# Another order for the attention weights of layer 1: when ScalarE rectifies and exponentiates, and when VectorE masks

## The chip, the cores and the metric

The kernel runs on one core of one Trainium2 chip. The metric is the device time of one launch in microseconds (us); lower is better. Everything is computed in that one launch, from inputs in the chip's memory to the output there.

## The reference, cut to what matters

A batch of 8 graphs with 1024 nodes and 256 features goes through four layers, each followed by a residual sum and a layer normalisation. Layer 0 averages neighbours, layer 1 is the one that the change touches, layer 2 is three graph convolutions, layer 3 is attention with 8 heads. Layer 1:

```python
Xw = X @ Wv + bv
sj = Xw @ aw[:d, 0]
si = Xw @ aw[d:, 0]
e = leaky_relu(sj[:, None, :] + si[:, :, None] + ab[0], negative_slope=0.2)
alpha_matrix = A * exp(e)
transition = alpha_matrix / (sum(alpha_matrix, axis=-1, keepdims=True) + 1e-12)
for k in range(3):
    H = H + Xk @ Wk[k] + bk[k]
    Xk = einsum('bij,bjd->bid', transition, Xk)
return relu(H)
```

So for each of 1024 queries there are 1024 weights: a rectified sum of a query's scalar `si` and a key's scalar `sj`, its exponential, and the product with the adjacency `A` (the masking). The sum over the keys divides the products later.

## The kernel before

One loop over the 8 batch elements holds all four layers. The nodes are cut into 8 tiles of 128. There is no scheduler: each engine has its own list of instructions in an order written out by hand, and semaphores tie the lists together. An engine runs its list strictly in order, so an instruction that waits holds all behind it. Matrix products are made of three: each operand is split into a high part (`t_hi`, `u_hi`, `xt_hi`) and a rest (`t_lo`, `u_lo`, `xt_lo`), and TensorE multiplies high by high, high by rest and rest by high (lines 506 to 508).

In the stage of the change, a weight tile is named (part, t), with t the tile of queries. Parts 0 and 1 are the keys 0 to 511 and 512 to 1023 of the query tiles 0 to 3 (128 x 512 values each: the short tiles); part 2 is all keys of the tiles 4 to 7 (128 x 1024: the wide tiles). The list `AL` gives their order: (0,0) to (0,3), (1,0) to (1,3), (2,4) to (2,7), 12 in all. A tile goes through these steps:

- ScalarE: `leaky(part, t)` (line 1049) adds `si_col` to `sj_row` and rectifies into `al_area`; `exponential(part, t)` (line 1054) works in place and waits for the rectified values. `leaky_exp` is the two in a row. A rectifier also waits until `si` of its query tile is there, and where it writes again into a used buffer, until the old tile has been transposed. The first of part 1 waits for the second half of `sj_row`.
- VectorE: `weights(part, t)` (line 1371) multiplies by the adjacency in place and sums the row, into `rsum_a` for part 0 and into `rsum` for the others.
- TensorE: `transpose_alpha(part, t)` (line 605), 4 transposes of 128 x 128 for a short tile and 8 for a wide one, into PSUM.
- ScalarE: `al_transposed(part, t)` copies PSUM to `t_hi` (all copies have line 931, that of a helper).
- VectorE: its own `al_transposed(part, t)` writes `t_lo`, PSUM less `t_hi` (line 1228).
- TensorE: `hop(part, t)` multiplies the weights with the value rows, 12 matmuls for a short tile and 24 for a wide one. The first of them waits for `t_lo`.

TensorE's list runs one transposition ahead: `transpose_alpha(0, 2)`, `hop(0, 1)`, `transpose_alpha(0, 3)`, `hop(0, 2)` and so on to `transpose_alpha(2, 4)`, `hop(1, 3)`, `transpose_alpha(2, 5)`, `hop(2, 4)`.

The value rows are the projection of the normalised input with the weights `W_K2`, in four pairs of tiles. VectorE takes each pair from PSUM with `both_rows(k)`: a cast to `u_hi` (line 1385) and the difference to `u_lo` (line 1228). Pairs 2 and 3 are first used by `hop(1, 0)`. `s_j()` on VectorE (line 1363) writes the second half of `sj_row`. `s_i(b, t)` (line 1308) is the product of a normalised tile with a weight row, summed over the features into `si_col`; its full-size output is scratch, in `y`, `xr` or `si_out`. The semaphore `si_done` counts these.

The copies into `t_hi` wait once for `t_out`: the transposed adjacency, which stands in the same place, must have been written out to memory by the SyncE queue (it is loaded back for layer 2). After the stage, VectorE forms the reciprocals of the row sums, and TensorE goes on to the projections `z` and to the second product with the same weights.

Of the kernel before, what the change touches and what calls it, by code (L numbers as in the profile page):

```python
# [22 lines left out]
def build_program(nc: bass.Bass, d: dict, out: bass.AP):  # L23
    B, N, F = d["x"].shape
    NT = N // P
# [63 lines left out]
    with ExitStack() as ctx:  # L89
        def sb(name, shape, dt=F32, stack=ctx):  # L90
            return stack.enter_context(nc.sbuf_tensor(name, shape, dt))

        def sem(name):
            return ctx.enter_context(nc.semaphore(name))
# [14 lines left out]
        wsi_row = sb("wsi_row", [P, F])  # L109
# [6 lines left out]
        xn = sb("xn", [P, NT, F])  # L116
# [19 lines left out]
        with ExitStack() as s:  # L136
            t_cols = sb("t_cols", [P, N - F], F32, s)
            si_out = sb("si_out", [P, F], F32, s)
# [24 lines left out]
        with ExitStack() as s:  # L163
# [6 lines left out]
            xr = sb("xr", [P, 2, F], F32, s)  # L170
# [14 lines left out]
        with ExitStack() as s:  # L185
            y = sb("y", [P, 4, F], F32, s)
# [8 lines left out]
        def al(part, t):  # L195

            if part == 2:
                return al_area[:, 1 + (t - 3) % 3, :]
            at = N + (TPH * part + t) % 6 * 512
            return al_area[:, :, :].rearrange("p k n -> p (k n)")[:, at:at + 512]  # L200
# [39 lines left out]
        si_done = sem("si_done")  # L240
# [43 lines left out]
        def nth(b, per, n):  # L284

            return b * per + n
# [40 lines left out]
        def al_banks(part, t):  # L327

            banks = BANKS[tp["al", part, t]]
            return ps[:, banks[0]:banks[-1] + 1, :].rearrange("p h (j i) -> p (h j) i", i=P)  # L330

        def al_keys(part):

            return slice(0, NT) if part == 2 else slice(TPH * part, TPH * (part + 1))

        def hop_place(t):

            return ps[:, ACC + t % 4, t // 4 * F:(t // 4 + 1) * F]
# [591 lines left out]
        def _(act):  # L930
# [79 lines left out]
            for b in range(B):  # L1010
# [23 lines left out]
                def leaky(part, t):  # L1034

                    n = AL.index((part, t))
                    act.wait_ge(si_done, nth(b, NT, t + 1))
                    if n == 0:
                        act.wait_ge(y_ready, nth(b, 3 * NT, NT))
                        act.wait_ge(sj_act, b + 1)  # L1040
                    if n == TPH:
                        act.wait_ge(pr_free, nth(b, PR_UNITS, pr["sj", 1] + 1))
                    if 6 <= n < 8:
                        act.wait_ge(tp_full, nth(b, TP_UNITS, tp["al", 0, n - 6] + 1))
                    elif n >= 8:
                        before = [("al", 0, 3), ("al", 1, 1), ("al", 1, 3), ("al", 2, 4)][n - 8]
                        act.wait_ge(tp_full, nth(b, TP_UNITS, tp[before] + 1))
                    row = sj_row[:, :] if part == 2 else sj_row[:, part * 512:(part + 1) * 512]
                    act.activation(al(part, t), row, ACT.Prelu, bias=si_col[:, t:t + 1], scale=1.0,
                                   alpha=SLOPE).then_inc(e_lin, 1)  # L1050

                def exponential(part, t):
                    act.wait_ge(e_lin, nth(b, len(AL), AL.index((part, t)) + 1))
                    act.activation(al(part, t), al(part, t), ACT.Exp).then_inc(e_exp, 1)

                def leaky_exp(part, t):
                    leaky(part, t)
                    exponential(part, t)

                def al_transposed(part, t):  # L1060
                    act.wait_ge(tp_full, nth(b, TP_UNITS, tp["al", part, t] + 1))
                    copy(t_hi[:, al_keys(part), t * P:(t + 1) * P], al_banks(part, t)).then_inc(tp_hi, 1)
# [10 lines left out]
                x_late_transposed(b, 1, 2)  # L1073
                exponential(0, 0)
                leaky_exp(0, 1)
                leaky(0, 2)
                act.wait_ge(t_out, nth(b, 32 * NT, 32 * NT))
                al_transposed(0, 0)
                exponential(0, 2)
                al_transposed(0, 1)  # L1080
                leaky_exp(0, 3)
                al_transposed(0, 2)
                leaky_exp(1, 0)
                al_transposed(0, 3)
                leaky_exp(1, 1)
                al_transposed(1, 0)
                leaky_exp(1, 2)
                al_transposed(1, 1)
                leaky_exp(1, 3)
                al_transposed(1, 2)  # L1090
                leaky(2, 4)
                al_transposed(1, 3)
                exponential(2, 4)
                leaky_exp(2, 5)
                for t in range(TPH, NT):
                    al_transposed(2, t)
                    if t + 2 < NT:
# [98 lines left out]
        def _(dve):  # L1196

            dve.wait_ge(set_in, SET_LOADS)
            for n, slot in enumerate((W_L0X, W_L0G, W_Q, W_K, W_V, W_O)):
                dve.wait_ge(set_act, n + 1)  # L1200
                scale = QSCALE if slot == W_Q else 1.0
                dve.scalar_tensor_tensor(out=w_lo[:, slot, :, :].rearrange("p k o -> p (k o)"),
                                         in0=ps[:, TP + n % 2, :], scalar=scale,
                                         in1=f32(w_hi[:, slot, :, :].rearrange("p k o -> p (k o)")),
# [17 lines left out]
            def alone():  # L1222

                dve.sem_inc(passed, 1)

            def rest(dst, value, hi, done):

                dve.tensor_tensor(dst, value, f32(hi), ALU.subtract).then_inc(done, 1)  # L1228
# [73 lines left out]
            def s_i(b, t):  # L1302

                dve.wait_ge(ln_done, nth(b, LN_PER, t + 1))
                if t == NT - 1:
                    dve.wait_ge(si_done, nth(b, NT, NT - 1))
                alone()
                dve.tensor_tensor_reduce(out=y[:, t % 4, :] if t < NT - 3 else (xr[:, 0, :] if t == NT - 3 else si_out[:, :]), in0=xn[:, t, :], in1=wsi_row[:, :], scale=1.0, scalar=0.0,
                                         op0=ALU.mult, op1=ALU.add, accum_out=si_col[:, t:t + 1]).then_inc(si_done, 1)

            def hidden(b, c):
# [8 lines left out]
            for b in range(B):  # L1320
# [16 lines left out]
                for t in range(NT):  # L1337
# [4 lines left out]
                                             scalar=rdeg[:, t:t + 1], in1=ev[:, t % 2, 0:F], op0=ALU.mult,  # L1342
# [23 lines left out]
                def weights(part, t):  # L1366

                    dve.wait_ge(e_exp, nth(b, len(AL), AL.index((part, t)) + 1))
                    alone()
                    keys = slice(0, N) if part == 2 else slice(part * 512, (part + 1) * 512)  # L1370
                    dve.tensor_tensor_reduce(out=al(part, t), in0=al(part, t), in1=adjn[:, t, keys], scale=1.0, scalar=0.0,  # L1371
                                             op0=ALU.mult, op1=ALU.add,
                                             accum_out=(rsum if part else rsum_a)[:, t:t + 1]).then_inc(al_ready, 1)

                def al_transposed(part, t):

                    at = slice(t * P, (t + 1) * P)
                    dve.wait_ge(tp_hi, nth(b, TP_UNITS, tp["al", part, t] + 1))
                    rest(t_lo[:, al_keys(part), at], al_banks(part, t), t_hi[:, al_keys(part), at], tp_free)

                def both_rows(k):

                    n, at = pr["v", k], slice(k * 512, (k + 1) * 512)
                    dve.wait_ge(pr_full, nth(b, PR_UNITS, n + 1))
                    dve.tensor_copy(u_hi[:, at], ps[:, PR + n % 2, :]).then_inc(v_hi, 1)  # L1385
                    if k == 0:
                        dve.wait_ge(sj_act, b + 1)
                        dve.sem_inc(pr_free, 1)
                    dve.wait_ge(v_hi, nth(b, PAIRS, k + 1))
                    rest(u_lo[:, at], ps[:, PR + n % 2, :], u_hi[:, at], pr_free)  # L1390
# [7 lines left out]
                weights(0, 1)  # L1398
                s_j()
                al_transposed(0, 0)  # L1400
                s_i(b, NT - 3)
                both_rows(3)
                weights(0, 2)
                al_transposed(0, 1)
                weights(0, 3)
                al_transposed(0, 2)
                weights(1, 0)
                al_transposed(0, 3)
                weights(1, 1)
                al_transposed(1, 0)  # L1410
# [20 lines left out]
                for k in range(NT // 2 + 1):  # L1431
                    if k < NT // 2:
# [3 lines left out]
                        for s in range(2):  # L1436
                            t = 2 * k + s
                            last = dve.scalar_tensor_tensor(
                                out=ev[:, k % 2, 512 + s * F:512 + (s + 1) * F],
                                in0=hop_place(t), scalar=rdeg[:, t:t + 1],  # L1440
                                in1=ev[:, k % 2, s * F:(s + 1) * F], op0=ALU.mult, op1=ALU.add)
# [5 lines left out]
                for t in range(NT + 1):  # L1447
                    if t < NT:
# [7 lines left out]
                                                 scalar=rdeg[:, t:t + 1], in1=ev[:, t % 2, 0:F], op0=ALU.mult,  # L1456
# [45 lines left out]
                for k, part in enumerate(QK):  # L1502
# [4 lines left out]
                    if k == 7:  # L1507
# [5 lines left out]
                                             scalar=cols[:, 2 + m, ft:ft + 1], in1=f32(qk_place(part, u_hi, qk0_hi)),  # L1513
                                             op0=ALU.add, op1=ALU.subtract).then_inc(pr_free, 1)
                stacks_copied(range(G + 1, 3 * G + 2, 2))
                for s in range(UNITS + 13):
                    if s < UNITS:
# [4 lines left out]
                        if s >= 4:  # L1522
# [3 lines left out]
                            out=r[:, s % RSLOTS, :], in0=ps[:, 2 * (s % 2):2 * (s % 2) + 2, :].rearrange("p a c -> p (a c)"),  # L1526
                            in1=adjn[:, qt, :], scale=1.0, scalar=-3.0e38, op0=ALU.mult, op1=ALU.max,
# [73 lines left out]
```

## Time and profile before

| | before |
|---|---|
| time, median of 3 runs | 3142.06 us (3141.99 to 3142.89) |
| the profiled execution | 3141.49 us, span 3139.7 us |
| TensorE matmul busy (PE) | 3023.2 us, 96% |
| TensorE weight load busy (PEld) | 2645.5 us, 84% |
| VectorE busy (DVE) | 2090.6 us, 67% |
| ScalarE busy (ACT) | 1724.4 us, 55% |
| GpSimd busy (POOL) | 448.6 us, 14% |
| mean granted TensorE clock | 0.992 of full speed |
| DMA | 234.50 MB, mean 75 GB/s |

The profile is of one execution. Its span is the time from the first to the last instruction, 1.8 us under the time of that execution. Busy time of an engine says how much work it has, not whether the end waits for it; matmuls are pipelined, so a start every 0.12 us with a duration of 0.28 us each is normal. What is decisive for an engine that is nearly always busy are its gaps: the views of the waits and of the timeline show how long it stood idle before an instruction and what released it. "L605" is line 605 of the kernel; an instruction's text gives the tile written, then the tiles read, their shapes, and how many were merged in one row.

### The profile page before, as it was taken

What the parts mean: (1) busy time and instruction counts of PE and PEld (TensorE: products, weight loads), DVE (VectorE), ACT (ScalarE), POOL (GpSimd) and SP (SyncE); (2) the same over time, 40 slices, a digit from 0 to 9 for tenths busy, and PEclk for the clock granted to TensorE, in tenths of its full rate; (3) what the DMA queues carried; (4) which work ended last, traced back from release to release, by engine and by line L of the source; (5) the groups of instructions that cost most, each with busy time, mean ns of one, the idle gap of its engine ahead of it and who ended that gap; (6) DMA issues with size and microseconds to landing.
All of it is one profiled execution on the core that took longest, in us unless ns stands there. A gap on an engine that the chain in (4) does not pass through costs nothing.

```text
span 3139.7 us, 71133 instructions
## 1 busy us (share of the span) xinstructions
PE 3023.2 (96%) x28188; PEld 2645.5 (84%) x28188; DVE 2090.6 (67%) x4060; ACT 1724.4 (55%) x3048; POOL 448.6 (14%) x1666
## 2 busy tenths in 40 slices
PE   6999999999999999999999999999999999999999
PEld 5988789877898788987889877898778987789877
DVE  4637976379762797627976389753887538874388
ACT  3525855258542684526844278442784337853377
POOL 0101211012110121101211012111121111211112
PEclk9999999999999999999999999999999999999999
DMA  5022131121321213202133021330213302133010
GB/s 218 30 79 65 49 145 54 57 70 44 144 77 37 67 52 135 96 22 67 49 135 108 12 71 44 134 108 14 69 52 125 108 14 72 49 125 108 24 42 19
DMA packets 145270, 234.50 MB, mean 75 GB/s; under 512 B 12839, under 2 KB 113964, under 8 KB 144940
## 3 DMA queue, kind: packets, MB, share of 16 engines
q1 hardware_dynamic: 144940, 229.96, 22.3%
q8 instruction: 225, 3.69, 0.5%
q14 instruction: 105, 0.86, 0.1%
HBM read 120.86 MB, written 83.89 MB: 65 GB/s over the span
## 4 chain that ended last, share of the span: by engine, by line
PE 87%; DVE 7%; ACT 3%; issue 2%; SPq 1%; POOL 1%; DMA 0%; DVEq 0%; POOLq 0%; ACTq 0%
PE ps L506 16%; PE ps L508 16%; PE ps L507 16%; PE ps L734 15%; PE ps L724 9%; PE ps L752 8%; PE ps L605 1%; DVE t_lo L1228 1%; PE ps L765 1%; PE ps L564 1%; PE ps L595 1%; DVE al_area L1371 1%; DVE u_hi L1385 1%; ACT t_hi L931 1%; PE ps L705 0%
## 5 line engine op out<-in xcount | busy, mean ns | idle before, releaser
L1525 DVE CUSTOM_DVE_ANT_0 r<-ps,adjn 128x1024 f32<-128x1024 f32 x512 | 620.7, 1212 | 18.9 <-DVE xr L1572 10.3
L1172 ACT ACTIVATE r<-r,nmax 128x1024 f32<-128x1024 f32 x512 | 584.8, 1142 | 23.0 <-POOL nmax L498 22.3
L506 PE MATMUL ps<-u_hi,t_hi 128*128 128x256 f32 x2048 | 588.6, 287 | 0.6
L508 PE MATMUL ps<-u_hi,t_lo 128*128 128x256 f32 x2048 | 579.3, 283 | 0.0
L507 PE MATMUL ps<-u_lo,t_hi 128*128 128x256 f32 x2048 | 578.9, 283 | 0.0
L734 PEld LDWEIGHTS ps<-ident,r 128*128 128x128 f32 x4096 | 462.5, 141 | 115.4 <-issue 77.4
L734 PE MATMUL ps<-ident,r 128*128 128x128 f32 x4096 | 536.8, 274 | 7.2 <-DVE pt L1541 7.0
L1541 DVE COPY pt<-ps 128x512 f32<-128x512 f32 x512 | 352.9, 689 | 93.4 <-PE ps L734 73.8
L931 ACT ACTIVATE pt<-ps 128x512 f32<-128x512 f32 x512 | 304.0, 594 | 176.5 <-PE ps L734 158.2
L506 PEld LDWEIGHTS ps<-u_hi,t_hi 128*128 128x128 f32 x2048 | 391.5, 191 | 4.0 <-DVE t_lo L1228 4.0
L507 PEld LDWEIGHTS ps<-u_lo,t_hi 128*128 128x128 f32 x2048 | 391.4, 191 | 0.0
L508 PEld LDWEIGHTS ps<-u_hi,t_lo 128*128 128x128 f32 x2048 | 391.2, 191 | 0.0
L724 PE MATMUL ps<-k_stack,q_stack 96*128 96x512 f32 x1024 | 363.3, 437 | 6.2 <-ACT k_stack L931 4.3
L1006 ACT ACTIVATE xn<-y,shift,rstd 128x256 f32<-128x256 f32 x192 | 115.6, 602 | 456.7 <-POOL shift L474 455.9
L506 PE MATMUL ps<-w_hi,xt_hi 128*128 128x256 f32 x1152 | 334.2, 290 | 18.1 <-DVE xt_lo L1235 8.2
L507 PE MATMUL ps<-w_lo,xt_hi 128*128 128x256 f32 x1152 | 322.8, 280 | 0.0
L508 PE MATMUL ps<-w_hi,xt_lo 128*128 128x256 f32 x1152 | 322.5, 280 | 0.0
L467 POOL TENSOR_TENSOR vare<-mv,eps_ln 128x1 f32<-128x1 f32 x256 | 53.5, 209 | 1607.6 <-DVE mv L1289 1607.6
L752 PE MATMUL ps<-pt,xn 128*32 128x128 f32 x8192 | 274.9, 275 | 0.0
L1228 DVE TENSOR_TENSOR xt_lo<-ev,xt_hi 128x512 fp32r<-128x512 f32 x64 | 44.3, 693 | 316.4 <-ACT xt_hi L931 316.4
L506 PEld LDWEIGHTS ps<-w_hi,xt_hi 128*128 128x128 f32 x1152 | 218.2, 189 | 35.6 <-issue 12.5
L498 POOL TENSOR_TENSOR nmax<-zero,mmax 128x1 f32<-128x1 f32 x512 | 97.1, 190 | 1036.7 <-DVE mmax L1525 1013.8
(165 smaller groups left out, 5237.2 us busy)
## 6 DMA issues: line engine op xcount, KB each, us to landing
adjn<-in_adj SPq DMA_DIRECT2D x64, 512.0 KB, 3.4
t_spill<-t_hi SPq DMA_DIRECT2D x64, 512.0 KB, 5.9
t_spill<-t_lo SPq DMA_DIRECT2D x64, 512.0 KB, 6.0
t_hi<-t_spill SPq DMA_DIRECT2D x32, 1024.0 KB, 5.4
t_lo<-t_spill SPq DMA_DIRECT2D x32, 1024.0 KB, 8.1
xn<-in_x SPq DMA_DIRECT2D x16, 512.0 KB, 4.2
x_spill<-xn SPq DMA_DIRECT2D x64, 128.0 KB, 1.7
q_stack<-u_hi SPq DMA_DIRECT2D x64, 128.0 KB, 2.5
```

What stands on the lines that cost most here:

```text
L498: pool.tensor_tensor(nmax[:, u % 4:u % 4 + 1], zero[:, :], mmax[:, u % 4:u % 4 + 1], ALU.subtract).then_inc(neg_max, 1)
L506: pe.matmul(dst, a_hi, b_hi, start=first, stop=False, skip_group_check=check)
L507: pe.matmul(dst, a_hi, b_lo, start=False, stop=False, skip_group_check=check)
L508: return pe.matmul(dst, a_lo, b_hi, start=False, stop=last, skip_group_check=check)
L724: last = pe.matmul(ps[:, 2 * (u % 2) + half, :], q_stack[0:STACK, h, qt * P:(qt + 1) * P], k_stack[0:STACK, h, half * 512:(half + 1) * 512 ...
L734: last = pe.transpose(ps[:, TP + half, t * P:(t + 1) * P], r[:, u % RSLOTS, (TPH * half + t) * P:(TPH * half + t + 1) * P], ident)
L752: last = pe.matmul(ps[HD * hh:HD * (hh + 1), ctx_bank(grp), g * P:(g + 1) * P], xn[:, kt, h * HD:(h + 1) * HD], p_half(grp * G + hh, kt // ...
L931: copy = lambda dst, src, scale=1.0: nc.scalar.activation(dst, src, ACT.Copy, scale=scale)
L1006: act.activation(dst, src, ACT.Identity, bias=shift[:, t % 4:t % 4 + 1], scale=rstd[:, t % 4:t % 4 + 1]).then_inc(ln_done, 1)
L1172: act.activation(r[:, s % RSLOTS, :], r[:, s % RSLOTS, :], ACT.Exp, bias=nmax[:, s % 4:s % 4 + 1], accum_out=prow[:, qt % 2, h:h + 1]).the ...
L1525: dve.tensor_tensor_reduce(out=r[:, s % RSLOTS, :], in0=ps[:, 2 * (s % 2):2 * (s % 2) + 2, :].rearrange("p a c -> p (a c)"), in1=adjn[:, q ...
L1541: dve.tensor_copy(p_half(u, 0).rearrange("p t q -> p (t q)"), ps[:, TP, :]).then_inc(p_dve, 1)
```

## The change

On ScalarE, the steps of the short tiles and of the first two wide ones come in another order. Before, most tiles have `leaky_exp` in one piece between two copies. After, (0,2) is done in full and (0,3) rectified before the first copy; from there each gap between two copies holds the exponential of one tile and the rectifier of the next. (2,4) is rectified ahead of copy (1,1) and exponentiated ahead of copy (1,2), (2,5) rectified ahead of copy (1,3) and exponentiated behind it.

On VectorE, `both_rows(3)` goes from ahead of `weights(0, 2)` to behind `weights(0, 3)`, and `s_i(b, NT - 3)` from ahead of `both_rows(3)` to behind `weights(1, 0)`. The scratch output of `s_i(b, NT - 3)` goes to `si_out`, as that of the two after it, no longer to `xr`; so `s_i(b, NT - 2)` too waits for the one before it. No instruction on data is added or taken away, and TensorE's, GpSimd's and SyncE's lists are as they were.

```diff
--- before.py
+++ after.py
@@ -1073,25 +1073,30 @@
                 x_late_transposed(b, 1, 2)
                 exponential(0, 0)
                 leaky_exp(0, 1)
-                leaky(0, 2)
+                leaky_exp(0, 2)
+                leaky(0, 3)
                 act.wait_ge(t_out, nth(b, 32 * NT, 32 * NT))
                 al_transposed(0, 0)
-                exponential(0, 2)
+                exponential(0, 3)
+                leaky(1, 0)
                 al_transposed(0, 1)
-                leaky_exp(0, 3)
+                exponential(1, 0)
+                leaky(1, 1)
                 al_transposed(0, 2)
-                leaky_exp(1, 0)
+                exponential(1, 1)
+                leaky(1, 2)
                 al_transposed(0, 3)
-                leaky_exp(1, 1)
+                exponential(1, 2)
+                leaky(1, 3)
                 al_transposed(1, 0)
-                leaky_exp(1, 2)
+                exponential(1, 3)
+                leaky(2, 4)
                 al_transposed(1, 1)
-                leaky_exp(1, 3)
+                exponential(2, 4)
                 al_transposed(1, 2)
-                leaky(2, 4)
+                leaky(2, 5)
                 al_transposed(1, 3)
-                exponential(2, 4)
-                leaky_exp(2, 5)
+                exponential(2, 5)
                 for t in range(TPH, NT):
                     al_transposed(2, t)
                     if t + 2 < NT:
@@ -1302,10 +1307,10 @@
             def s_i(b, t):
 
                 dve.wait_ge(ln_done, nth(b, LN_PER, t + 1))
-                if t == NT - 1:
-                    dve.wait_ge(si_done, nth(b, NT, NT - 1))
+                if t > NT - 3:
+                    dve.wait_ge(si_done, nth(b, NT, t))
                 alone()
-                dve.tensor_tensor_reduce(out=y[:, t % 4, :] if t < NT - 3 else (xr[:, 0, :] if t == NT - 3 else si_out[:, :]), in0=xn[:, t, :], in1=wsi_row[:, :], scale=1.0, scalar=0.0,
+                dve.tensor_tensor_reduce(out=y[:, t % 4, :] if t < NT - 3 else si_out[:, :], in0=xn[:, t, :], in1=wsi_row[:, :], scale=1.0, scalar=0.0,
                                          op0=ALU.mult, op1=ALU.add, accum_out=si_col[:, t:t + 1]).then_inc(si_done, 1)
 
             def hidden(b, c):
@@ -1398,13 +1403,13 @@
                 weights(0, 1)
                 s_j()
                 al_transposed(0, 0)
-                s_i(b, NT - 3)
-                both_rows(3)
                 weights(0, 2)
                 al_transposed(0, 1)
                 weights(0, 3)
+                both_rows(3)
                 al_transposed(0, 2)
                 weights(1, 0)
+                s_i(b, NT - 3)
                 al_transposed(0, 3)
                 weights(1, 1)
                 al_transposed(1, 0)
```

## Rows read from the trace of the kernel before

**Rows 1.** The page: busy time and share by engine; the last chain by engine.

```profile
PE 3023.2 (96%) x28188; PEld 2645.5 (84%) x28188; DVE 2090.6 (67%) x4060; ACT 1724.4 (55%) x3048; POOL 448.6 (14%) x1666
...
PE 87%; DVE 7%; ACT 3%; issue 2%; SPq 1%; POOL 1%; DMA 0%; DVEq 0%; POOLq 0%; ACTq 0%
```

**Rows 2.** TensorE's waits, whole span: who waited for whom, us in total, times, longest.

```profile
PE ps L605 <- DVE rsum L1371: 13.0, 8, 1.6
...
PE ps L605 <- DVE rsum_a L1371: 4.4, 8, 0.6
```

**Rows 3.** TensorE's timeline, third element: start, us, instruction, count, idle before and its releaser.

```profile
874.75 0.60 PE L605 MATMUL ps<-ident,al_area 128*128 128x128 f32 x4
...
875.10 0.37 PE L506 MATMUL ps<-u_hi,t_hi 128*128 128x256 f32 x1
...
877.31 0.66 PE L605 MATMUL ps<-ident,al_area 128*128 128x128 f32 x4 [0.54 <-DVE rsum_a L1371]
...
877.91 0.39 PE L506 MATMUL ps<-u_hi,t_hi 128*128 128x256 f32 x1
...
879.45 0.60 PE L605 MATMUL ps<-ident,al_area 128*128 128x128 f32 x4
...
886.91 0.60 PE L605 MATMUL ps<-ident,al_area 128*128 128x128 f32 x4
...
890.56 1.09 PE L605 MATMUL ps<-ident,al_area 128*128 128x128 f32 x8 [1.63 <-DVE rsum L1371]
...
892.92 1.03 PE L605 MATMUL ps<-ident,al_area 128*128 128x128 f32 x8
...
894.04 0.39 PE L506 MATMUL ps<-u_hi,t_hi 128*128 128x256 f32 x1
...
897.01 1.03 PE L605 MATMUL ps<-ident,al_area 128*128 128x128 f32 x8
...
897.81 0.36 PE L506 MATMUL ps<-u_hi,t_hi 128*128 128x256 f32 x1
```

**Rows 4.** ScalarE's timeline, third element.

```profile
865.79 0.60 ACT L1006 ACTIVATE xn<-y,shift,rstd 128x256 f32<-128x256 f32 x1 [3.96 <-POOL shift L474]
...
866.30 0.67 ACT L1068 ACTIVATE sj_row<-ps,e_const 128x512 f32<-128x512 f32 x1
...
871.19 0.63 ACT L1054 ACTIVATE al_area<-al_area 128x512 f32<-128x512 f32 x1
...
871.73 0.71 ACT L1049 ACTIVATE al_area<-sj_row,si_col 128x512 f32<-128x512 f32 x1
...
873.41 0.60 ACT L931 ACTIVATE t_hi<-ps 128x512 fp32r<-128x512 f32 x1 [0.98 <-PE ps L605]
...
873.91 0.62 ACT L1054 ACTIVATE al_area<-al_area 128x512 f32<-128x512 f32 x1
...
886.17 1.14 ACT L1049 ACTIVATE al_area<-sj_row,si_col 128x1024 f32<-128x1024 f32 x1
...
887.54 0.60 ACT L931 ACTIVATE t_hi<-ps 128x512 fp32r<-128x512 f32 x1 [0.23 <-PE ps L605]
...
888.04 1.05 ACT L1054 ACTIVATE al_area<-al_area 128x1024 f32<-128x1024 f32 x1
```

**Rows 5.** VectorE's timeline, third element.

```profile
873.63 0.75 DVE L1363 TENSOR_SCALAR sj_row<-ps,e_const 128x512 f32<-128x512 f32 x1
...
875.23 0.69 DVE L1385 CAST u_hi<-ps 128x512 fp32r<-128x512 f32 x1
...
876.56 0.68 DVE L1371 CUSTOM_DVE_ANT_0 al_area<-al_area,adjn 128x512 f32<-128x512 f32 x1
...
877.17 0.69 DVE L1228 TENSOR_TENSOR t_lo<-ps,t_hi 128x512 fp32r<-128x512 f32 x1
...
877.77 0.68 DVE L1371 CUSTOM_DVE_ANT_0 al_area<-al_area,adjn 128x512 f32<-128x512 f32 x1
...
889.27 1.23 DVE L1371 CUSTOM_DVE_ANT_0 al_area<-al_area,adjn 128x1024 f32<-128x1024 f32 x1 [2.10 <-ACT al_area L1054]
```

## What I expect of the change, and why

> **What bounds the kernel now.** I read the page's busy shares and its chain by engine first [rows 1]: TensorE is busy 96% of the span and carries 87% of the chain that ended last. Time can come out only where TensorE stands still. The view of who waited for whom, for TensorE, then gives the stops of the edited stage [rows 2]: the transposes of line 605 waited for VectorE's `rsum` 8 times, 13.0 us in all, and for its `rsum_a` 8 times, 4.4 us in all. Eight is once per batch element, and the longest single waits (1.6 us, 0.6 us) are about the means, so all elements behave alike. I follow the third one, by TensorE's timeline [rows 3], then ScalarE's [rows 4] and VectorE's [rows 5], because a wait says who came last, not why.
>
> I write T(p,t) for a tile's transposes on TensorE, hop(p,t) for its matmuls, leaky, exp and copy for ScalarE's three steps, w for VectorE's masking and rest for its `t_lo` subtraction. With nothing late a short cycle (T, then a hop) takes (886.91 - 879.45) / 4 = 1.865 us, its T 0.35 of it (874.75 to 875.10), so its hop 1.515. A wide T takes 0.80 (897.01 to 897.81). Against these TensorE loses [rows 3]:
> - First wait: T(0,2) could start at 875.10 + 1.515 = 876.62 and starts at 877.31: 0.69.
> - hop(0,1) follows 0.60 behind that T, not 0.35: 0.25.
> - Second wait: T(2,4) could start at 886.91 + 1.865 = 888.78 and starts at 890.56: 1.78.
> - hop(2,4) starts at 894.04, where 892.92 + 0.80 = 893.72 was possible: 0.32.
>
> Together 3.04 us an element, 24.3 us over eight: no reordering in this stage can gain more.
>
> **Why the long wait is there.** ScalarE starts leaky(2,4) at 886.17, then copies (1,3) at 887.54, for which it waits until T(1,3) is done, and only then runs exp(2,4), 888.04 to 889.09 [rows 4]. w(2,4) follows at 889.27 and takes 1.23 [rows 5]; T(2,4) starts 0.06 later [rows 3]. So the exponential stands behind a copy that cannot be early.
>
> **The ScalarE edit, step by step.** No instruction is added or removed; 12 rectifiers, 12 exponentials and 12 copies stay. Start to start, one behind the other [rows 4]: exp to the next 0.54 (871.19 to 871.73), copy to the next 0.50 (873.41 to 873.91), leaky to its own exp 0.74, since it waits for that result (871.19 + 0.54 + 0.74 gives the exp of the new order at 872.47). The new order also has leaky followed by a copy. Before shows this pair only where the copy waited for TensorE (886.17 and 887.54 in [rows 4]), with 0.23 us idle at most; an upper bound is that it costs as much as to its own exp, 0.74, a lower one is what another ScalarE step with column operands shows: the normalisation of 0.60 is followed after 0.51 (865.79, 866.30), an overlap of 0.09, so 0.71 - 0.09 = 0.62. I take 0.62, as that row is the same kind of instruction without a wait.
>
> The Trainium skill, "ScalarE: Activation LUTs", section "What ACT_TABLE_LOAD costs", says that back-to-back ACTIVATEs overlap by about 93 ns, which is what the row of the normalisation shows; by that rule the sum is the one with 0.62, and without it the one with 0.74 below.
>
> From leaky(0,2) at 871.73 [rows 4]: exp(0,2) 872.47, leaky(0,3) 873.01, copy(0,0) 873.63. That copy is 0.22 later than before. Its rest started at 874.29, 0.60 + 0.03 behind the copy's end is 874.26, so what follows is not later. Then exp(0,3) 874.13, and leaky(1,0) 874.67, which now stands ahead of copy(0,1) and needs the second half of `sj_row`: VectorE writes it 873.63 to 874.38 [rows 5], cover 0.29. copy(0,1) starts at 875.39, right behind T(0,1) (874.75 + 0.60), as before.
>
> **The VectorE edit.** Before, `s_i(b, NT - 3)` and the value pair (`both_rows(3)`: cast at 875.23, its difference, next instruction at 876.56, so 1.33) stand ahead of w(0,2), 876.56 to 877.24 [rows 5], and that is the first wait. After, w(0,2) follows rest(0,0) at 874.90 (exp(0,2) was done at 873.10) and ends at 875.58, over 1 us before TensorE could use it. rest(0,1) at 876.02 (copy end 875.99) ends at 876.71: hop(0,1) can start at 876.97. Both losses go, 0.94. What is late next: w(0,3) at 876.62 takes 0.61 to the next instruction, then the value pair 1.33, so rest(0,2) starts at 878.56 and ends at 879.25; hop(0,2) could start at 876.62 + 1.865 + 0.35 = 878.83 and gets its data at about 879.30. A new wait of 0.47, behind the moved pair. Net of this edit with the ScalarE edit: hop(0,2) at 879.30, where before T(0,3) at 879.45 puts it at 879.80, a gain of 0.50. The value pair is needed first by hop(1,0) four cycles on; `s_i(b, NT - 3)` only by leaky(2,5). The extra wait on `si_done` ahead of `s_i(b, NT - 2)` is for an instruction several steps back; w(1,2), next in line behind it, ends some 0.8 us before T(1,2) needs it. No DMA and nothing of SyncE or GpSimd moves; the SyncE queue waits for TensorE's later products and shifts with them.
>
> **The rest of the stage.** From hop(0,2) at 879.30 the cycles run at 1.865: T(1,0) 880.82, T(1,1) 882.68, T(1,2) 884.55, T(1,3) 886.42, T(2,4) 888.29. Does w(2,4) keep up? ScalarE's short cycle is 0.62 + 0.50 + 0.54 = 1.66 (1.78 by the upper bound), under 1.865. exp(2,4) comes at about 884.0 and ends at 885.1, ahead of copies (1,2) and (1,3). VectorE needs 0.60 for a rest and 0.61 for a w [rows 5], is free of rest(1,2) at 886.42 and ends w(2,4) at 887.65, 0.64 ahead of need. The second wait goes; T(2,4) is 890.56 - 888.29 = 2.27 earlier. copy(1,3) starts 0.65 behind T(1,3), at 887.07; exp(2,5) follows at 887.57, 1.05 long, then w(2,5) 0.18 later, 888.81 to 890.04; T(2,5) wants it at 888.29 + 0.80 + 1.515 = 890.61, cover 0.57. At hop(2,4) the way of a wide tile (T, copy, rest) took 894.04 - 890.56 = 3.48 before; TensorE's own work in it is 0.80 + 1.515 + 0.80 = 3.12. This wait stays, 0.31 to 0.36. From there the orders agree. hop(2,4) comes at 891.72, a gain of 2.32 an element.
>
> **The sum.** 8 x 2.32 = 18.6 us. The profiled execution took 3141.49 us (span 3139.7); after, 3122.9. The median of the runs is 3142.06, 0.6 above, which gives 3123.5. With 0.74 for leaky to copy, copies (0,1), (0,2) and (1,1) come up to 0.3 late, the gain is 2.10 an element, 16.8 us, and the time is 3125.3. TensorE's granted clock is 0.992 of full speed on the mean of the span, so next to always at the higher of its two levels; idle time only goes away, and I cost the clock at nothing.
>
> **Rivals.**
> 1. *The moved pair eats the first gain.* If rest(0,2) is late by 0.5 more than I work out (VectorE reading TensorE's banks more slowly when denser work runs, or copy(0,1) late behind leaky(1,0), whose cover is 0.29), only the second wait is won: 8 x 1.78 = 14.2, 3127.9. For it: VectorE has no slack between 876.0 and 879.3 in the new order. Against: each step is a duration read in this stage.
> 2. *Both waits go with no new one.* Adds 8 x 0.47: 22.3, 3119.8. Against: 0.47 has to be made up on a full VectorE.
> 3. *The work moved makes no difference to the end:* the time is given back later, at a transfer or at the products behind the stage. [Rows 2] has no transfer that this stage's TensorE work waits for. About 3142, within 6 us.
> 4. *Slower: ScalarE becomes the bound.* If a rectifier, an exponential and a copy no longer run pairwise but cost more one by one, as with a change of function, the copies hold every hop. The point at which the whole gain is gone is a ScalarE cycle of 1.865 + 2.32 / 8 = 2.16 where I have 1.66; each 0.1 beyond costs 8 x 8 x 0.1 = 6.4 us. A step to 2.4 gives some 3157. Against: 871.19 to 871.73, 873.41 to 873.91 and the 0.23 idle at most at 887.54 [rows 4] are such changes, and none shows a pause.
>
> The same page of the Trainium skill, section "Table sets: the hidden batching unit", tells to batch by table set since a switch costs about 2.7 us; that would speak for the fourth rival by far, but the pairs in these rows show no such switch.
>
> **How the numbers follow.** Forecast 0.71, first rival 0.16, second 0.04, third 0.05, fourth 0.04. Predicted 3123.5. A change of under 0.2% (6.3 us) can't be told from none here. The forecast's own range is 3121 to 3126; with the first two rivals' ends the range is 3119.7 to 3128.2. Faster 0.71 + 0.16 + 0.04 = 0.91, same 0.05, slower 0.04.
>
> **What would show it.** After: no wait of line 605 for `rsum` or `rsum_a`; in its place a wait of line 506 for `t_lo`, some 0.5 us an element at hop(0,2), plus the 0.3 at hop(2,4) that stays; copies spaced 1.87 in the short cycles; `al_area` of (2,4) exponentiated before copy(1,2). Wrong if line 605 still waits for VectorE, or if `t_lo` waits appear in several cycles per element.

## The result and the profile after

| | before | after |
|---|---|---|
| time, median of 5 runs | 3142.06 us (3141.32 to 3143.99) | 3125.73 us (3123.78 to 3131.49) |
| the profiled execution, span | 3141.49 us, 3139.7 us | 3123.78 us, 3122.0 us |
| the stage, in each element | 34.45 to 34.47 us | 32.08 to 32.13 us |

The ratio is 0.995, with a 95% interval of 0.9938 to 0.9962: faster, by 16.3 us on the medians and 17.7 us between the two profiled executions. Timed again beside the kernel before, the changed one took 3123.62 us against 3142.66 (ratio 0.9937, 0.9925 to 0.995). "The stage" is here and below the time from the start of the activation that writes the first half of `sj_row` (line 1068) to the first transpose of the last wide tile, T(2,7). It is read from the two timelines, as the mean of the 8 elements, and is the length that the change acts on.

The page of the changed kernel: its span, the busy times, and the chain that ended last by engine.

```profile
span 3122.0 us, 71133 instructions
...
PE 3021.2 (97%) x28188; PEld 2645.0 (85%) x28188; DVE 2089.0 (67%) x4060; ACT 1718.1 (55%) x3048; POOL 448.6 (14%) x1666
...
PE 87%; DVE 5%; ACT 3%; SPq 2%; issue 1%; POOL 1%; DMA 0%; DVEq 0%; POOLq 0%; ACTq 0%
```

TensorE runs the same 28188 matmuls with 2.0 us less of busy time, in a span 17.7 us shorter; the gain is idle time. TensorE's waits, who waited for whom, us in total, times and longest:

```profile
PE ps L564 <- DVE t_lo L1233: 23.4, 8, 3.2
...
PE ps L506 <- DVE t_lo L1233: 1.8, 8, 0.3
```

Line 605 has no row any more, where [rows 2] had 13.0 and 4.4 us. A wait of line 506 for `t_lo` is new, once per element. The other wait, at line 564, was there before and has nothing to do with the stage. TensorE's timeline of the third element (in all timelines: start, us, instruction, count, idle before and its releaser; beside [rows 3]):

```profile
871.57 0.60 PE L605 MATMUL ps<-ident,al_area 128*128 128x128 f32 x4
...
873.44 0.60 PE L605 MATMUL ps<-ident,al_area 128*128 128x128 f32 x4
...
873.79 0.36 PE L506 MATMUL ps<-u_hi,t_hi 128*128 128x256 f32 x1
...
875.31 0.60 PE L605 MATMUL ps<-ident,al_area 128*128 128x128 f32 x4
...
876.12 0.39 PE L506 MATMUL ps<-u_hi,t_hi 128*128 128x256 f32 x1 [0.22 <-DVE t_lo L1233]
...
877.65 0.60 PE L605 MATMUL ps<-ident,al_area 128*128 128x128 f32 x4
...
883.25 0.60 PE L605 MATMUL ps<-ident,al_area 128*128 128x128 f32 x4
...
885.12 0.71 PE L605 MATMUL ps<-ident,al_area 128*128 128x128 f32 x5
...
887.43 0.71 PE L605 MATMUL ps<-ident,al_area 128*128 128x128 f32 x5
...
888.53 0.38 PE L506 MATMUL ps<-u_hi,t_hi 128*128 128x256 f32 x1
...
891.50 0.71 PE L605 MATMUL ps<-ident,al_area 128*128 128x128 f32 x5
```

The figure x4 or x5 counts the transposes that the view merged in one row. The rows are T(0,1), T(0,2), the start of hop(0,1), T(0,3), the start of hop(0,2), T(1,0), T(1,3), T(2,4), T(2,5), the start of hop(2,4), T(2,6). T(0,2) follows T(0,1) after 1.87 and T(2,4) follows T(1,3) after 1.87, a plain cycle both times: the two long waits are gone. hop(0,2) starts 0.81 behind T(0,3), where 0.35 would do, and hop(2,4) 1.10 behind T(2,5), where 0.80 would do. The view of the waits shows less of this than the distances from start to start: it has 0.22 us at hop(0,2), where the start is 0.46 late, and nothing at hop(2,4), since the ends of the matmuls ahead are modelled. The distances are what counts here.

ScalarE (beside [rows 4]):

```profile
869.83 0.71 ACT L1049 ACTIVATE al_area<-sj_row,si_col 128x512 f32<-128x512 f32 x1
...
870.45 0.58 ACT L931 ACTIVATE t_hi<-ps 128x512 fp32r<-128x512 f32 x1
...
880.82 1.06 ACT L1054 ACTIVATE al_area<-al_area 128x1024 f32<-128x1024 f32 x1
...
882.02 0.60 ACT L931 ACTIVATE t_hi<-ps 128x512 fp32r<-128x512 f32 x1
...
883.89 0.60 ACT L931 ACTIVATE t_hi<-ps 128x512 fp32r<-128x512 f32 x1 [0.23 <-PE ps L605]
```

leaky(0,3) to copy(0,0) takes 0.62. exp(2,4) runs at 880.82, ahead of copies (1,2) and (1,3), which are the last two rows. VectorE (beside [rows 5]): w(0,2), w(0,3), the cast of the last value pair, rest(0,2), w(2,4).

```profile
871.72 0.68 DVE L1376 CUSTOM_DVE_ANT_0 al_area<-al_area,adjn 128x512 f32<-128x512 f32 x1
...
873.45 0.68 DVE L1376 CUSTOM_DVE_ANT_0 al_area<-al_area,adjn 128x512 f32<-128x512 f32 x1
...
874.05 0.69 DVE L1390 CAST u_hi<-ps 128x512 fp32r<-128x512 f32 x1
...
875.38 0.68 DVE L1233 TENSOR_TENSOR t_lo<-ps,t_hi 128x512 fp32r<-128x512 f32 x1
...
883.26 1.22 DVE L1376 CUSTOM_DVE_ANT_0 al_area<-al_area,adjn 128x1024 f32<-128x1024 f32 x1
```

w(0,2) now ends over 1 us ahead of T(0,2). Between w(0,3) and rest(0,2) stands the value pair, and rest(0,2) ends at 876.06, 0.06 ahead of the late hop(0,2). w(2,4) ends at 884.48, 0.64 ahead of T(2,4).

### The profile page after: what moved, and what is told of

It is laid out like the page before. It is cut to its first block, busy times and chain, and to the rows that moved or that the text cites. A ratio compares the mean times of both kernels' runs of the same rounds, so it can differ in the third digit from the quotient of the medians.

```text
span 3122.0 us, 71133 instructions
## 1 busy us (share of the span) xinstructions
PE 3021.2 (97%) x28188; PEld 2645.0 (85%) x28188; DVE 2089.0 (67%) x4060; ACT 1718.1 (55%) x3048; POOL 448.6 (14%) x1666
## 4 chain that ended last, share of the span: by engine, by line
PE 87%; DVE 5%; ACT 3%; SPq 2%; issue 1%; POOL 1%; DMA 0%; DVEq 0%; POOLq 0%; ACTq 0%
PE ps L506 17%; PE ps L508 16%; PE ps L507 16%; PE ps L734 15%; PE ps L724 9%; PE ps L752 8%; DVE t_lo L1233 2%; SPq L409 1%; PE ps L605 1%; PE ps L765 1%; PE ps L564 1%; ACT t_hi L931 1%; PE ps L595 1%; DVE xt_lo L1240 0%; DVE stats L1289 0%
```

## The experiments

All stages are the means over the 8 elements of the profiled execution. Times are medians, and "before" is the median of the kernel before on the same chip; the rows come from two chips, so gains are to be compared by the ratios and not by the medians.

| kernel | stage, us | time, us | before, us | ratio, 95% interval |
|---|---|---|---|---|
| before | 34.46 | | | |
| after | 32.11 | 3123.62 | 3142.66 | 0.9937 (0.9925 to 0.995) |
| ScalarE's order alone | 32.60 | 3126.94 | 3141.71 | 0.9951 (0.9938 to 0.9965) |
| VectorE's order alone | 34.76 | 3144.32 | 3141.71 | 1.0009 (1.0 to 1.0018) |
| value pair parted | 31.63 | 3117.69 | 3141.71 | 0.9924 (0.9911 to 0.9936) |
| one swap in the kernel before | 34.03 | 3137.45 | 3141.71 | 0.9985 (0.9977 to 0.9994) |
| after, ScalarE loaded | 33.36 | 3133.98 | 3142.66 | 0.9969 (0.9958 to 0.9981) |
| value pair parted, wide tile in halves | 31.37 | 3118.66 | 3142.66 | 0.9922 (0.9908 to 0.9935) |

**ScalarE's order alone.** The kernel before with the new ScalarE list of the diff.

> Only ScalarE's new order; VectorE's list as before. The stage is measured from the start of the first `sj_row` activation to the last wide T of an element: 34.46 us before, 32.11 after the whole change. My theory (each wait is the meeting of three in-order lists; the two edits are not additive): the first wait stays as it is (T(0,2) about 0.7 late, hop(0,1) 0.24), the second, at T(2,4), goes, hop(2,4) keeps 0.3. Stage 32.6, gain 1.87 an element, 15 us in all, about 3127. Rival (the long wait needs both edits, since VectorE's masking comes late): T(2,4) still waits for over 0.5, stage over 33.1.

The stage is 32.60, as worked out. TensorE's waits of line 605:

```profile
PE ps L605 <- DVE rsum_a L1376: 4.4, 8, 0.6
```

The wait for `rsum_a`, the first one, is whole (4.4 us), and the wait for `rsum`, the second one, is gone, without VectorE's edit. 1.86 of the 2.35 us an element is ScalarE's.

**VectorE's order alone.** The kernel before with the new VectorE list and the scratch place that goes with it.

> Only VectorE's new order (and the scratch place that goes with it); ScalarE's list as before. My theory: T(0,2) is no longer late, but exp(0,3) still stands behind copy(0,1), so w(0,3), the value pair behind it and then rest(0,2) are late, and hop(0,2) waits 1.3; the second wait stays whole. Stage 34.8, slower than before by 0.3 an element, 3 us in all, about 3145. Rival (additive: the first wait belongs to VectorE's order alone): stage 33.5 to 34.0, 4 to 8 us faster.

The stage is 34.76, 0.30 longer than before; on the totals the interval reaches 1.0, so 2.6 us slower is at the edge of what they tell, and the stage tells it in all 8 elements (34.74 to 34.80). The waits:

```profile
PE ps L605 <- DVE rsum L1371: 13.0, 8, 1.6
...
PE ps L506 <- DVE t_lo L1228: 8.3, 8, 1.0
```

The wait for `rsum_a` is gone and one for `t_lo` has come in its place, 8.3 us where 4.4 went. ScalarE (copy(0,1), leaky(0,3), exp(0,3)), VectorE (w(0,3), rest(0,2)) and TensorE (T(0,3), hop(0,2)) show the way:

```profile
877.38 0.60 ACT L931 ACTIVATE t_hi<-ps 128x512 fp32r<-128x512 f32 x1 [0.80 <-PE ps L605]
...
877.88 0.71 ACT L1049 ACTIVATE al_area<-sj_row,si_col 128x512 f32<-128x512 f32 x1
...
878.62 0.63 ACT L1054 ACTIVATE al_area<-al_area 128x512 f32<-128x512 f32 x1
```

```profile
879.43 0.69 DVE L1371 CUSTOM_DVE_ANT_0 al_area<-al_area,adjn 128x512 f32<-128x512 f32 x1 [0.73 <-ACT al_area L1054]
...
881.38 0.68 DVE L1228 TENSOR_TENSOR t_lo<-ps,t_hi 128x512 fp32r<-128x512 f32 x1
```

```profile
880.49 0.60 PE L605 MATMUL ps<-ident,al_area 128*128 128x128 f32 x4
...
882.12 0.39 PE L506 MATMUL ps<-u_hi,t_hi 128*128 128x256 f32 x1 [1.03 <-DVE t_lo L1228]
```

exp(0,3) stands behind copy(0,1) and ends at 879.25; w(0,3) starts 0.18 later, the value pair behind it, and rest(0,2) ends at 882.06. So hop(0,2) starts 1.63 behind its T. VectorE's half of the edit is worth 0.49 on top of ScalarE's (32.60 to 32.11) and costs 0.30 without it. This half moves two things, `s_i(b, NT - 3)` and the value pair, and no run moves one alone. By [rows 5] the pair alone would do for the first wait: w(0,2) would then start at 875.23 and end at 875.91, ahead of the 876.62 at which T(0,2) could start. That is an estimate.

**The last value pair parted.** The changed kernel, with `both_rows(3)` cut in its two instructions, the cast (`high_rows`) and the difference (`low_rows`):

```diff
                 weights(0, 2)
+                high_rows(3)
                 al_transposed(0, 1)
                 weights(0, 3)
-                both_rows(3)
+                low_rows(3)
                 al_transposed(0, 2)
```

> The changed kernel with one more step: the last value pair's two instructions on VectorE are parted, the cast goes to where VectorE waits for copy(0,1) (behind w(0,2)), the difference stays behind w(0,3). My theory: the 0.47 at hop(0,2) is the cast's place in VectorE's line and nothing else; it goes, no new wait comes. Stage 31.65, 0.47 less than after the change, 3.7 us in all, about 3121. Rival (VectorE simply has too much work between two hops): the wait moves to hop(0,3) or hop(1,0), stage 32.0 to 32.2.

The stage is 31.63, and the wait for `t_lo` at line 506 has no row left. VectorE (w(0,2), cast, rest(0,1), w(0,3), the pair's difference, rest(0,2)), then TensorE (T(0,3), hop(0,2)):

```profile
869.70 0.68 DVE L1376 CUSTOM_DVE_ANT_0 al_area<-al_area,adjn 128x512 f32<-128x512 f32 x1
...
870.30 0.68 DVE L1390 CAST u_hi<-ps 128x512 fp32r<-128x512 f32 x1
...
870.91 0.68 DVE L1233 TENSOR_TENSOR t_lo<-ps,t_hi 128x512 fp32r<-128x512 f32 x1
...
871.50 0.68 DVE L1376 CUSTOM_DVE_ANT_0 al_area<-al_area,adjn 128x512 f32<-128x512 f32 x1
...
872.11 0.68 DVE L1233 TENSOR_TENSOR u_lo<-ps,u_hi 128x512 fp32r<-128x512 f32 x1
...
872.72 0.68 DVE L1233 TENSOR_TENSOR t_lo<-ps,t_hi 128x512 fp32r<-128x512 f32 x1
```

```profile
873.23 0.60 PE L605 MATMUL ps<-ident,al_area 128*128 128x128 f32 x4
...
873.58 0.36 PE L506 MATMUL ps<-u_hi,t_hi 128*128 128x256 f32 x1
```

The cast fills the time in which VectorE waited for copy(0,1), and hop(0,2) starts 0.35 behind its T. The pair also costs less in two pieces, 0.61 and 0.61, where together it took 1.33: the difference waits for the cast's result, and right behind it that wait shows. So the new wait of the changed kernel was one instruction's place, not too much work on VectorE.

**One swap.** The kernel before, with the exponential taken ahead of the copy that stood in front of it:

```diff
                 leaky(2, 4)
-                al_transposed(1, 3)
                 exponential(2, 4)
+                al_transposed(1, 3)
                 leaky_exp(2, 5)
```

> The kernel before with a single swap: exp(2,4) ahead of copy(1,3), nothing else. My theory: the exponential comes only 0.7 earlier, since ScalarE is behind already (its short cycle of 1.78 leaves 0.09 of TensorE's 1.865), so T(2,4) still waits about 1.1 and copy(1,3), now late, makes w(2,5) and T(2,5) wait 0.3. Stage 34.0, gain 0.45 an element, 3 to 4 us in all, about 3138. Rival (the long wait is that one swap): stage about 32.7, over 12 us faster.

The stage is 34.03. T(1,3), T(2,4) and T(2,5):

```profile
885.76 0.60 PE L605 MATMUL ps<-ident,al_area 128*128 128x128 f32 x4
...
888.73 0.77 PE L605 MATMUL ps<-ident,al_area 128*128 128x128 f32 x5 [0.95 <-DVE rsum L1371]
...
891.34 0.77 PE L605 MATMUL ps<-ident,al_area 128*128 128x128 f32 x5
```

T(2,4) comes 2.97 behind T(1,3), where 1.865 would do, so it is late by 1.11 instead of 1.78, and T(2,5) comes 2.61 behind T(2,4), where 0.80 + 1.515 = 2.32 would do. The copy that the timeline shows ahead of the late exponential is little over a third of the 1.78; the rest is that ScalarE arrives at leaky(2,4) with no lead, and the run with ScalarE's order alone, where T(2,4) follows T(1,3) after 1.87, shows that a lead removes all of it.

**ScalarE loaded.** The changed kernel with more work on ScalarE in part 1:

```diff
+                    if part == 1:
+                        copy(al(part, t), row).then_inc(extra, 1)
+                        act.wait_ge(extra, 4 * b + t + 1)
                     act.activation(al(part, t), row, ACT.Prelu, bias=si_col[:, t:t + 1], scale=1.0,
```

> The changed kernel with more work on ScalarE: ahead of each rectifier of part 1 a plain copy of the same size into the buffer that the rectifier then overwrites, and a wait for it; by the durations of after about 0.65 us more in each of four short cycles. The result is the same. My theory: ScalarE's cycle of 1.66 has only 0.2 to spare against TensorE's 1.865, so these 2.6 us make several hops wait (hop(0,1), (0,2), (0,3), (1,0), (1,1), together about 1.7 more than after), and the last idle of ScalarE takes up the rest. Stage 33.5, against 32.11, 11 us in all, about 3137. Rival (VectorE alone is the limit in the new order, ScalarE has slack): stage 32.1 to 32.4, under 3 us.

The stage is 33.36: 1.25 longer than after, for about 2.6 us of work. ScalarE's cycle, from copy(0,1) over exp(1,0), the added copy and leaky(1,1) to copy(0,2):

```profile
874.77 0.58 ACT L932 ACTIVATE t_hi<-ps 128x512 fp32r<-128x512 f32 x1
...
875.25 0.62 ACT L1058 ACTIVATE al_area<-al_area 128x512 f32<-128x512 f32 x1
...
875.77 0.62 ACT L932 ACTIVATE al_area<-sj_row 128x512 f32<-128x512 f32 x1
...
876.42 0.72 ACT L1053 ACTIVATE al_area<-sj_row,si_col 128x512 f32<-128x512 f32 x1
...
877.05 0.58 ACT L932 ACTIVATE t_hi<-ps 128x512 fp32r<-128x512 f32 x1
```

It is 2.28 long, against TensorE's 1.865, and no step of it is idle. The loss was expected as 1.4, 0.14 too much. This is the fourth rival's mechanism made real: where ScalarE's cycle goes above TensorE's, the hops wait, and 1.66 leaves 0.2.

**The first wide tile in halves.** On top of the parted pair, ScalarE copies (2,4) in two halves of 512, and VectorE subtracts the first while the second is copied:

```diff
+                    if (part, t) == (2, TPH):
+                        at = slice(t * P, (t + 1) * P)
+                        copy(t_hi[:, 0:TPH, at], al_banks(part, t)[:, 0:TPH, :]).then_inc(first_hi, 1)
+                        copy(t_hi[:, TPH:NT, at], al_banks(part, t)[:, TPH:NT, :]).then_inc(tp_hi, 1)
+                        return
```

(VectorE's `al_transposed` likewise.)

> The previous kernel with the parted value pair, and the first wide tile (2,4) copied and subtracted in two halves of 512, so that VectorE starts on the first while ScalarE copies the second. My theory: the 0.3 at hop(2,4) is the length of the line T, copy, rest (3.43 against TensorE's own 3.12 in it); by halves it is about 2.95, and the wait goes. Stage 31.3 to 31.4, 0.75 less than after the change, 6 us in all, about 3119. Rival (the two more instructions on each engine, about 0.1 each, cost at T(2,6) what they give): stage 31.6 to 31.7.

T(2,5), hop(2,4), T(2,6), hop(2,5):

```profile
885.19 0.71 PE L606 MATMUL ps<-ident,al_area 128*128 128x128 f32 x5
...
885.98 0.36 PE L507 MATMUL ps<-u_hi,t_hi 128*128 128x256 f32 x1
...
888.94 0.71 PE L606 MATMUL ps<-ident,al_area 128*128 128x128 f32 x5
...
889.79 0.39 PE L507 MATMUL ps<-u_hi,t_hi 128*128 128x256 f32 x1
```

hop(2,4) starts 0.79 behind T(2,5), so its wait is gone; hop(2,5) has 0.05 of a new one. The stage is 31.37. The first totals (3118.66 against 3117.69, beside different runs of before) did not show it, so the two were run again side by side.

> The kernel with the parted value pair, side by side with the one with halves on the same chip. Stage 31.63 as in its first run. Median 3116 to 3121.

> The kernel with the parted value pair and the first wide tile in halves, on the same chip. Stage 31.36, 0.27 an element less, so 2.2 us less by the stages; the medians should differ by that if enough runs average out the stretch between elements, whose length varies by about 2 us from element to element in every kernel. Rival: no difference or slower by the totals, as in the first comparison (3117.69 and 3118.66), which would mean that the halves cost elsewhere what they give here.

Stages 31.63 and 31.36; medians 3117.16 (3115.95 to 3118.32) and 3116.22 (3111.98 to 3117.35), ratios to before 0.9922 (0.9909 to 0.9934) and 0.9913 (0.99 to 0.9927). Over the 8 elements the stages differ by 2.2 us in sum; the totals now point the same way, where the first comparison pointed the other, and can't confirm it. Both beat the changed kernel. Against the kernel before on the same chip the parted pair gained 24.0 and 24.4 us and the kernel with halves 24.0 and 25.4, where the changed kernel gained 16.3 and 19.0; by the stages they should gain 3.8 and 5.9 us more than it. What exceeds that is not explained by the stage.

**The changed kernel again.**

> The changed kernel itself, timed again beside the kernel before. The stage is 32.11 in every element. If the scatter of its times (3123.8 to 3131.5, against 2.7 us for the kernel before) lies between the end of attention and the next element's first products, where TensorE's granted clock falls in some elements, then the stretches outside that one repeat within 0.1 us here too, and the median may be anywhere from 3122 to 3128. Rival (the new order itself varies): the stage's length differs between elements by over 0.3.

The stage was 32.06 to 32.14 in all elements, so the new order itself doesn't vary. From T(2,7) to the first scores of layer 3 it was 150.57 to 150.63. From there to the next element's stage the lengths were 200.98 to 202.68. That stretch holds the scatter, in every kernel. Over the first five kernels' profiles (before, after twice, parted, ScalarE alone), 35 such stretches, its length goes with the granted clock of 20 us around the end of an element: about 201.0 on the mean of the three where no drop shows (1.00), 202.0 at 0.91, 202.5 at 0.83. But within the level of 0.91 alone the lengths run from 200.96 to 203.21, so the clock can't be the whole of it. Two such stretches of the changed kernel, the shortest (200.44) and the longest (203.21), each 20 us from 148.04 behind the first scores on; columns are the stretch, its length, busy time and instructions of PE, PEld, DVE, ACT and POOL, granted clock, DMA share, GB/s:

```profile
1193.90:1213.90 20.00, 15.13 (x122) 13.77 (x123) 14.21 (x26) 12.09 (x24) 1.94 (x7) 1.00 0.81 311
...
2731.60:2751.60 20.00, 14.67 (x106) 12.90 (x106) 14.03 (x28) 10.96 (x22) 2.73 (x9) 0.91 0.74 276
```

In both, TensorE is idle for a quarter of the time and DMA carries the next adjacency. The counts of instructions show that the two windows don't hold the same work: the longer stretch is already 1.9 us behind where its window starts, so their GB/s can't be set against each other.

Counting TensorE's matmuls (transposes among them) from the first scores on gives pieces of equal work, and two of them hold 2.4 of the 2.77 us.

- *The first 80, at the start of layer 3:* 12.53 us in the shorter stretch, 14.07 in the longer, at the full clock in both. In the longer one TensorE waits twice here for VectorE's `pt` (line 1546), 1.2 us together; the shorter has no such wait over 0.13 us.
- *The 60 from number 1901 on, around the end of the element:* 11.78 us at a clock of 1.00 over the 20 us, 12.68 at 0.91. A matmul takes 0.282 us on the mean in the one and 0.314 in the other, TensorE's idle time is shorter in the longer one (3.50 against 3.95 us), and DMA moves 250 and 260 GB/s. So this part goes with the clock: the matmuls themselves run longer, and DMA is no slower.

The eleven profiles bear this out, in the 75 of their 77 stretches that show the same number of matmuls. The second piece takes 11.73 to 11.79 us at 1.00 (5 stretches), 12.18 to 12.68 at 0.91 (51) and 13.07 to 13.42 at 0.83 (19), with nothing in between. The first piece takes 12.53 to 14.14, whatever the clock does later. The two pieces between them vary by 0.4 us each, and the last 39 us before the next stage by 0.1. What makes VectorE late at the start of layer 3 no run here tells. Nor does any trace show the slowest execution of the changed kernel, 3131.49 us, which was not profiled.

## Why the prediction was right, point by point

- *TensorE's gaps are the only source.* Right: the instructions are the same, and of the stage's 2.35 us an element (34.46 to 32.11) 2.28 are the gaps that went and came (0.69 + 0.25 + 1.78 - 0.46 + 0.02). The prediction left out a small one: behind the late T(2,4) the next T came after 2.36 ([rows 3], 890.56 to 892.92), where 0.80 + 1.515 = 2.32 would do; after the change it comes after 2.31. So the 3.04 us that it called the most a reordering could gain were some 0.05 too low; parted pair and halves together gain 3.09, though the halves add instructions.
- *First wait.* T(0,2) late by 0.69 and hop(0,1) by 0.25: both gone. The new wait at hop(0,2) was forecast at 0.47; it is 0.81 - 0.35 = 0.46. Its cause was named right too: parting the value pair removed it.
- *Leaky to copy, between 0.62 and 0.74.* Measured 0.62 at copy(0,0). The rule of the Trainium skill about back-to-back activations ("ScalarE: Activation LUTs", section "What ACT_TABLE_LOAD costs") holds in this trace: 0.71 for the rectifier, 0.62 to the next start. No pause at a change of function shows either.
- *Second wait.* Forecast gone, with w(2,4) 0.64 ahead; measured 0.64. The ScalarE list alone removes it.
- *hop(2,4) keeps 0.31 to 0.36.* Measured 1.10 - 0.80 = 0.30, just under that.
- *Gain of 2.32 an element.* Measured 2.35; over eight, 18.8 us against 18.6.
- *The total.* Forecast 3122.9 for a profiled execution and 3123.5 for the median; measured 3123.78 and 3125.73. What differs lies outside the stage. Between the two profiled executions the stages gave 18.83 us. Of the rest, the start of the first stage came 1.48 later (94.36 against 92.88), the stretch behind the last T(2,7) took 0.6 more, the middle parts 0.2 more and the seven stretches between elements 1.1 less, about half of it in each of the two pieces named above: 17.7 in all. The prediction counted these at nothing and had no range for them. In the eleven profiles the span less the eight stages is 2862.9 to 2866.5 us, 2864.0 in the kernel before and 2864.6 on the mean of the ten others, so nothing is a fair mean and some 2 us either way would have been a fair range for one execution; the profile before already showed the stretches between elements to differ by 1.9 us. The first median of five came out 2.2 us above the forecast, near the upper end of its own range (3121 to 3126), the second, 3123.62, 0.1 above. How near a single median falls is luck.
- *The rivals.* The first (only the second wait is won, 14.2 us) didn't come; ScalarE's list alone is close to it, 1.86 x 8 = 14.9. The second (no new wait) did not come with this change and is what the parted pair does: 8 x 2.83 = 22.6 us by the stages, where it was put at 22.3. The third is out: of the 18.8 us that the stages gained, 17.7 arrived at the end of the profiled execution, and the rest is within the scatter outside them. The fourth needs a ScalarE cycle of 2.16; loaded to 2.28 in four cycles the kernel was still faster than before (0.9969). Only four of the eight short cycles were loaded; an estimate for all eight, 8 x (2.28 - 1.865) = 3.3 us an element, is more than the whole gain of 2.35.
- *What I did not say:* that VectorE's edit alone is slower than the kernel before. The prediction costed both edits in one order, and its statement of the first wait reads as if VectorE's list alone removed it. The run shows that it only does so together with exp(0,3) ahead of the first copy.

## What to carry to other kernels

Where each engine follows its own fixed list, write down the start of each step on each engine for one round, with intervals read from the trace; here that gave the stage's length within 0.05 us for the change and five further variants, and within 0.14 us for the one with added work. Ask of a late instruction how much lead its engine has there: moving it past one neighbour won 0.43 of 1.78 us, while building up a lead some cycles earlier won all. Two halves of a reordering are not additive, and an instruction that is not yet needed belongs where its engine waits anyway.

## What the runs showed of the hardware

- An activation of 512 columns right behind another starts 0.09 to 0.10 us before that one's end when it doesn't need its result, for a rectifier (0.71, next start 0.62), an exponential (0.63, 0.54) and a copy (0.60, 0.50) alike; a rectifier's own exponential, which needs its result, starts after 0.74, 0.12 later. On VectorE a cast and the difference that needs it cost 1.33 as a pair and 1.22 with another instruction between them.
- The stretch from the first scores of layer 3 to the next element's stage, the same instructions each time, took 200.44 to 203.33 us over all runs. One source is the granted clock around the end of the element, where TensorE is idle for a quarter of the time: the same 60 matmuls take 11.8, 12.3 or 13.2 us on the mean with the clock at 1.00, 0.91 or 0.83 over 20 us. The other lies at the start of layer 3, 190 us before the next stage and at the full clock, where TensorE waits for VectorE, 1.2 us in the longest such stretch of the changed kernel and not at all in the shortest. A gain below some 2 us in total is seen in the stage and not in a median of five.
